# A macaron block on one core: the first stage turns most of its rows with a round trip to memory and 32x32 block transposes on VectorE, where TensorE did it

## What is computed

```
x = x + 0.5 * ffn(layernorm(x))
x = x + attn(layernorm(x))
x = x + 0.5 * ffn(layernorm(x))

ffn(y):   dots = softmax(y @ centroids.T / 0.1); hits = dots > 0.01      # 64 clusters
          query_sel = any(hits, axis=1); row_sel = any(hits, axis=0)[assignments]
          out = where(query_sel[:, None] & row_sel[None, :], y @ weight.T + bias, 0)
attn(y):  q, k, v = y @ Wq + bq, y @ Wk + bk, y @ Wv + bv                # 32 heads of 32, 8 key/value heads
          per token: scores[d, e] = sum over heads of q[d, h] k[e, h] / sqrt(32); softmax over e; times v
```

## Time and profile before

| | |
|---|---|
| median of 3 runs | 1314.02 us (1314.0 to 1318.34) |
| the profiled execution: its own time | 1314.43 us |
| its span in the profile | 1312.6 us, 21943 instructions |
| busy: PE, DVE, ACT, POOL | 1253.2, 837.8, 411.5, 437.1 us |
| share of the chain that ended last | PE 86%, DVE 9%, DMA 2% |
| moved by DMA | 178.91 MB, mean 136 GB/s |
| DMA packets under 512 bytes | 141312 of 197605 |

### The profile page before, as it was taken

The page is one execution under the profiler, slowest core; times in us unless marked ns, Lnnn a source line. Parts: engine busy times, 40 slices in busy tenths (PEclk is TensorE's granted clock), DMA queues, the critical chain, the costliest instruction groups (busy, mean ns, idle before and its releaser), DMA issues.

```text
span 1312.6 us, 21943 instructions
## 1 busy us (share of the span) xinstructions
PE 1253.2 (95%) x8776; PEld 1077.6 (82%) x8776; DVE 837.8 (64%) x1177; ACT 411.5 (31%) x590; POOL 437.1 (33%) x548
## 2 busy tenths in 40 slices
PE   5999999999999798999999999999999999979998
PEld 4788888888888677888888888888888888858887
DVE  3643343334333267888888887878888875198886
ACT  3322222222221123444344344444344443211110
POOL 1225443544231733324323433333333200051321
PEclk9999999999999898999999999999999999989999
DMA  7132333233212244555555545545545555116774
GB/s 256 53 116 89 128 108 118 89 128 100 78 65 112 73 112 112 162 153 145 146 142 132 155 132 154 164 132 147 158 123 154 137 136 187 47 67 223 271 272 177
DMA packets 197605, 178.91 MB, mean 136 GB/s; under 512 B 141312, under 2 KB 163840, under 8 KB 197504
## 3 DMA queue, kind: packets, MB, share of 16 engines
q1 hardware_dynamic: 182624, 158.11, 39.8%
q10 hardware_dynamic: 14880, 19.40, 4.3%
HBM read 103.55 MB, written 73.92 MB: 135 GB/s over the span
## 4 chain that ended last, share of the span: by engine, by line
PE 86%; DVE 9%; DMA 2%; issue 1%; POOL 1%; ACT 1%; SPq 1%; DVEq 0%; POOLq 0%
PE ps_b L257 12%; PE ps_b L259 12%; PE ps_b L258 12%; PE ps_a L257 11%; PE ps_a L259 10%; PE ps_a L258 10%; PE ps_t L264 6%; PE ps_s L1283 4%; DVE probs L1041 3%; PE ps_s L271 3%; PE ps_s L273 2%; PE ps_s L1333 2%; DVE odd_lo L992 1%; PE ps_s L278 1%; DVE qkv_tok L1036 1%
## 5 line engine op out<-in xcount | busy, mean ns | idle before, releaser
L257 PE MATMUL ps_a<-w_hi,odd_hi 128*128 128x512 f32 x464 | 187.0, 403 | 0.0
L259 PE MATMUL ps_a<-w_hi,odd_lo 128*128 128x512 f32 x464 | 182.3, 393 | 0.0
L258 PE MATMUL ps_a<-w_lo,odd_hi 128*128 128x512 f32 x464 | 182.1, 392 | 0.0
L257 PE MATMUL ps_b<-proj_hi,y_hi 128*128 128x256 f32 (+1 forms) x512 | 177.9, 347 | 0.0
L259 PE MATMUL ps_b<-proj_hi,y_lo 128*128 128x256 f32 (+1 forms) x512 | 172.6, 337 | 0.0
L258 PE MATMUL ps_b<-proj_lo,y_hi 128*128 128x256 f32 (+1 forms) x512 | 172.0, 336 | 0.0
L567 POOL TENSOR_SCALAR f_out<-f_out,token_on 128x1024 f32<-128x1024 f32 x31 | 88.6, 2857 | 173.8 <-DVE f_out L896 173.8
L291 POOL TENSOR_TENSOR var_eps<-moments,eps 128x1 f32<-128x1 f32 x96 | 18.4, 192 | 364.1 <-DVE moments L287 364.1
L613 POOL TENSOR_TENSOR f_tmp<-f_tmp,mask 128x1024 f32<-128x1024 f32 x32 | 72.7, 2273 | 146.9 <-DMA f_tmp<-f_scratch 146.9
L259 PEld LDWEIGHTS ps_b<-proj_hi,y_lo 128*128 128x128 f32 x512 | 97.1, 190 | 10.8
L896 DVE TENSOR_TENSOR f_out<-ps_b,bias_a 128x512 f32<-128x512 f32 x30 | 20.7, 691 | 132.9 <-PE ps_b L259 132.9
(11 more groups left out here) (181 smaller groups left out, 2783.1 us busy)
## 6 DMA issues: line engine op xcount, KB each, us to landing
xa<-in_L_attn_x SPq DMA_DIRECT2D x32, 512.0 KB, 5.6
f_tmp<-f_scratch SPq DMA_DIRECT2D x32, 512.0 KB, 5.0
x_ring<-in_L_attn_x SPq DMA_DIRECT2D x32, 512.0 KB, 4.2
f_scratch<-f_out SPq DMA_DIRECT2D x31, 512.0 KB, 3.0
x_scratch<-x_ring SPq DMA_DIRECT2D x30, 512.0 KB, 3.3
late<-x_scratch SPq DMA_DIRECT2D x22, 512.0 KB, 6.7
qkv_scratch<-qkv_tok SPq DMA_DIRECT2D x32, 256.0 KB, 3.0
f_scratch<-f_out ACTq DMA_DIRECT2D x60, 128.0 KB, 3.5
```

Source lines behind the costliest of these rows:

```text
L257: pe.matmul(acc, hi[:, k, :], w_h[:, k, cols], start=(k == 0), stop=False)
L258: pe.matmul(acc, hi[:, k, :], w_l[:, k, cols], start=False, stop=False)
L259: last = pe.matmul(acc, lo[:, k, :], w_h[:, k, cols], start=False, stop=(k == KB - 1))
```

## The change

Tiles 0 to 3 (`BY_PE = 4`) are turned as before. For tiles 4 to 31:

- ACT normalises in place, in `xa[t % 3]`.
- SP stores the normalised tile to a new scratch tensor `y_d` in memory (`store_normed`, 512 KB). It then waits for that store, and loads the tile back to `ya_tok[t % 2]` in four DMAs (`load_blocks`). Each moves 1024 pieces of 32 values (128 bytes), so that the 32x32 blocks of the tile change places: block row b, block column (k, a) goes to partitions 32a to 32a+31, columns (k, b).
- DVE transposes each 32x32 block in place (`turn_first`), and signals `t1`. `high_first` and `low_first` read `ya_tok` instead of `ps_t`.
- PE's `transpose_first` is gone for these tiles. ACT's `high_first` waits for the product that last read its set, since no transpose on PE stands between any more.
- On DVE the first part of the softmax moves ahead of `low_first` of the even tile.
- On SP, a tile load into `xa` now waits for the store of the normalised tile that lay there (`y_stored`), and stores and block loads are placed between the tile loads and the stores of results. The first load of stage two waits for `lo1` instead of `t1`.
- Six semaphores of stage three are shared with stage one.

```diff
+BY_PE = 4
...
+    y_d = nc.dram_tensor("y_scratch", (NT, P, EMB), F32, kind="Internal").ap()
...
+        def first_turned(t):
+            return ps_t[:, :, :] if t < BY_PE else ya_tok[t % 2][:, :].rearrange("p (k n) -> p k n", n=P)
...
                 def load_first(t):
-                    wait(sp, y1, t - 2)
+                    if t - 3 < BY_PE:
+                        wait(sp, y1, t - 2)
+                    else:
+                        sp.wait_ge(y_stored, 16 * (t - 2 - BY_PE))
                     sp.dma_start(xa[t % 3][:, :], x_d[t]).then_inc(xa_in[t % 3], 16)
...
+                def store_normed(t):
+                    sp.wait_ge(y1, t + 1)
+                    sp.dma_start(y_d[t], xa[t % 3][:, :]).then_inc(y_stored, 16)
+
+                def load_blocks(t):
+
+                    sp.wait_ge(y_stored, 16 * (t + 1 - BY_PE))
+                    if t - 2 < BY_PE:
+                        sp.wait_ge(t1, t - 1)
+                    else:
+                        sp.wait_ge(lo1, t - 1)
+                    blocks = y_d[t].rearrange("(b i) (k a j) -> a i k b j", i=D, a=T4, j=D)
+                    for a in range(T4):
+                        sp.dma_start(ya_tok[t % 2][D * a:D * a + D, :].rearrange("i (k b j) -> i k b j", b=T4, j=D),
+                                     blocks[a]).then_inc(y_in[t % 2], 16)
...
                 for p in range(NP - 1):
                     if p > 0:
                         store_first(2 * p - 1)
-                    for t in (2 * p + 5, 2 * p + 6):
-                        if t < NT:
-                            load_first(t)
+                    if 2 * p + 5 < NT:
+                        load_first(2 * p + 5)
+                    if 2 * p + 4 < NT:
+                        store_normed(2 * p + 4)
+                        load_blocks(2 * p + 4)
+                    if 2 * p + 6 < NT:
+                        load_first(2 * p + 6)
                     if 1 <= p <= KB:
                         load_proj(p - 1, [w[(p - 1) * P:p * P].rearrange("p d h -> p (d h)") for w in (Wq, Wk, Wv)])
...
                     store_first(2 * p)
+                    if 2 * p + 5 < NT:
+                        store_normed(2 * p + 5)
+                        load_blocks(2 * p + 5)
...
                 def norm_first(t):
                     act.wait_ge(norm1, t + 1)
-                    wait(act, t1, t - 1)
-                    normed(act, ya_tok[t % 2][:, :], xa[t % 3][:, :], 0, t).then_inc(y1, 1)
+                    if t < BY_PE:
+                        wait(act, t1, t - 1)
+                    to = ya_tok[t % 2] if t < BY_PE else xa[t % 3]
+                    normed(act, to[:, :], xa[t % 3][:, :], 0, t).then_inc(y1, 1)
...
                 def high_first(t):
                     act.wait_ge(t1, t + 1)
-                    act.copy(first_set(t)[0], ps_t[:, :, :]).then_inc(hi1, 1)
+                    if t >= BY_PE:
+                        act.wait_ge(ffn1[1], t - 3)
+                    act.copy(first_set(t)[0], first_turned(t)).then_inc(hi1, 1)
...
+                def turn_first(t):
+                    dve.wait_ge(y_in[t % 2], 64 * ((t - BY_PE) // 2 + 1))
+                    dve.transpose(ya_tok[t % 2][:, :], ya_tok[t % 2][:, :]).then_inc(t1, 1)
...
                 for p in range(1, NP - 2):
                     read_first(2 * p - 1, 1)
+                    turn_first(2 * p + 2)
+                    pair_soft_in(dve, p)
                     low_first(2 * p + 2)
-                    pair_soft_in(dve, p)
                     pair_soft_out(dve, 0, p)
                     stats_first(2 * p + 4)
                     read_first(2 * p, 0)
+                    turn_first(2 * p + 3)
                     low_first(2 * p + 3)
                     read_first(2 * p, 1)
                     stats_first(2 * p + 5)
                     read_first(2 * p + 1, 0)
...
                 for p in range(1, NP - 2):
-                    transpose_first(2 * p + 2)
                     fold_pair(p)
                     product_first(2 * p, 0)
-                    transpose_first(2 * p + 3)
                     product_first(2 * p, 1)
```

More of the change, by code:

```diff
@@ L220, in macaron_kernel @@
         ye, te, hie, loe = sem("ye"), sem("te"), sem("hie"), sem("loe")
-        late_in = sems("late_in", 6)
+        late_in = w_in[0:6]
         yl, tl, hil, lol = sem("yl"), sem("tl"), sem("hil"), sem("lol")
@@ L408, in _ @@
                     store_first(2 * p)
-                sp.wait_ge(t1, NT)
+                    if 2 * p + 5 < NT:
+                        store_normed(2 * p + 5)
+                        load_blocks(2 * p + 5)
+                sp.wait_ge(lo1, NT)
                 sp.wait_ge(f1_stored[0], 16)
@@ L875, in low_first @@
                     dve.wait_ge(hi1, t + 1)
-                    dve.tensor_tensor(lo, ps_t[:, :, :], hi.bitcast(F32), ALU.subtract).then_inc(lo1, 1)
+                    dve.tensor_tensor(lo, first_turned(t), hi.bitcast(F32), ALU.subtract).then_inc(lo1, 1)
                 def low_rows(j):
@@ L947, in _ @@
                     read_first(2 * p + 1, 0)
+                turn_first(NT - 2)
+                pair_soft_in(dve, NP - 2)
                 low_first(NT - 2)
-                pair_soft_in(dve, NP - 2)
                 pair_soft_out(dve, 0, NP - 2)
                 read_first(NT - 5, 1)
+                turn_first(LAST)
                 low_first(LAST)
```

5 lines of the change are left out of this document (2 added, 3 removed).

## The result

| | before | after |
|---|---|---|
| median of 8 runs, us | 1314.01 (1306.53 to 1320.15) | 1307.08 (1301.29 to 1310.77) |
| ratio of the runs | | 0.9943, 95% interval 0.9916 to 0.9969 |
| profiled execution, us (span) | 1314.43 (1312.6) | 1301.29 (1299.5) |

The change makes the kernel 6.9 us faster. 16.0 were forecast: the sign is right, and the size is less than half of what was forecast. Single executions of either kernel differ by 9 to 14 us, as much as is to be explained, so the comparison needs a point that does not carry the variation of stages two and three. I take **the mark**: the start of the first transposes of stage two on PE. All the work that the change alters lies before it; behind it only six semaphores are other ones. It stands at 439.93 us before and at 431.96 after: **8.0 us earlier**.

What follows compares the result with a forecast made beforehand. PE was taken to bound stage one, sharing the bound with the DVE, POOL, ACT chain after the change. 23.4 - 5.9 - 1.5 = 16.0 us gained, so a median of 1298.0 us, range 1293 to 1326.

Steps and rivals of the forecast that it cites:

- the likeliest case: Whole kernel: the forecast of 1298.0 us holds, own range 1293 to 1304; chance 0.5.
- the first rival, the shared read: Even tile's low part held by POOL's selection, both reading SBUF: 0.75 us in 13 rounds, 9.8 us, time 1307.8; one in four.
- What goes from PE: Eight transposes per tile leave PE's list in stage one: 1.67 us a pair, 14 pairs, 23.4 us gained.
- The wait at `pair_first`: PE waits for the odd tile's low part, 0.45 us in each of 13 rounds, 5.9 us lost.
- Start: I put 1.5 us: Loop start: tile 4's blocks arrive at 60.7, 1.1 us late, tile 5 a little too; 1.5 us lost.
- The round trip in the steady rounds: Store 3.0 us, block loads 5.3 (bounds 3.8 to 10.6), hidden by slack in steady rounds.
- its own sign: Block loads in the profile after: under 7.8 us from first issue to last landing.
- The slack of the odd tile: Rounds with projection loads: blocks at 272.8, transpose may start at 275.3; slack 2.5 us, 1.2 with the worst store.
- a sign of being wrong: DVE's block transposes waiting for `ya_tok` loads in rounds with projection loads would show the forecast wrong; no size given.
- The rival of late blocks: Odd tile's blocks land later than 7.8 us in 8 projection-load rounds; up to 1325.7 us; chance 0.25.

Runs made afterwards that it cites:

- e12: e11 with tile 5's xa load in round 0 put back ahead of tile 4's y_scratch store: median 1293.94 us, ratio 0.9817 to the kernel before.
- e1: The change without the round trip: the norm writes ya_tok directly, no store or block loads, result wrong: mark 424.24, time 1297.76 us.
- e2: The change with six tiles instead of four turned by TensorE (BY_PE = 6): mark 425.94, time 1301.44 us.
- e9: The change with only SyncE's list reordered, y_scratch store ahead of xa load, projection loads and f_scratch store: mark 426.98, time 1301.61 us.
- e3: The change with ACT's odd high part ahead of the next tile's norm from round 1 on: mark 437.90, time 1311.92 us.
- e10: The change with GpSimd's selection written as a tensor_tensor and done twice in a row: mark 462.64, time 1342.63 us.
- e4: The change with the pair logits one product later in PE's list: mark 426.55, time 1299.14 us.
- e11: The kernel of e5, timed over 6 runs: median 1297.24 us, ratio 0.9869 to the kernel before.
- e5: The change with pair logits one product later and y_scratch stores ahead in SyncE's list: mark 418.63, time 1293.73 us in one execution.
- e7: e5 with six tiles instead of four turned by TensorE: mark 418.80, time 1299.40 us.
- e8: The change with GpSimd's selection as a tensor_tensor with broadcast operand instead of a tensor_scalar: mark 430.91, time 1307.41 us.

## Why the prediction was wrong

The median of 1307.1 lies inside the range of 1293 to 1326 and outside the likeliest case's own, 1293 to 1304. That it lies next to the 1307.8 of the first rival, the shared read, is chance: that rival's wait did not occur.

- **What goes from PE: right, a little low.** 1.67 us were summed for a pair. With no wait left a round takes 24.15, 1.79 less than 25.94. e12 gets 23.3 us at the mark, where the sum had 23.4.
- **The wait at `pair_first`: right.** 0.42 where 0.45 stood, set by ACT's norm ahead of the odd high part and not by the blocks (e1 has it without any blocks). But the idle time of a row is not the wait's cost, 0.69 (24.84 - 24.15). A round is 24.84 where 25.94 - 1.22 = 24.72 stood: 13 x 0.12 = 1.6 us.
- **"Start: I put 1.5 us": this is the step that failed.** It cost 7.2. The sum looked at tile 4 and gave tile 5 "a little". Tile 4 was usable at 63.15 instead of 60.7, and tile 5, which nothing had priced, at 73.62. Three sizes in it were wrong: the store was taken at 3.0 us, the median of the earlier trace rows, and took 4.1 and 6.55; a block DMA was taken at 0.43 us of SyncE and took 0.84 here; and the 4.3 us of stall brought 2.9 more by the clock, a term that the sum did not have. Besides, tile 5's store went out 1.25 us behind its norm, because SyncE had the blocks of tile 4, a tile load and a store of results to issue first. e1 (no trip) and e2 (a later first trip) show that the trip causes this loss; e9 shows that an earlier store takes away the wait at `pair_first`, of which a part comes back at `fold_pair`.
- **The round trip in the steady rounds: close, with less slack than stated.** The forecast was 5.3 us from the first issue to the last landing; it was 5.23 to 7.95, within the bounds of 3.8 and 10.6, and once above the 7.8 that the prediction gave as its own sign. The odd tiles' stores in rounds with projection loads took 4.9 to 5.3 us where the prediction had 4.3 (263.2 to 267.5), apart from the first at 7.8. The slack of the odd tile was forecast at 2.5 us in these rounds and was 0 to 1.4. Two transposes there did wait for `ya_tok` (0.37 and 0.30), which the prediction had named as a sign of being wrong, without cost to PE; the round with the bias vectors lost 0.5 us. e3, whose even tiles start their trip 1.05 us later, has seven rounds of over 25 us.
- Together: 5.7 at the start, 1.6 in the rounds, 0.5 in one round are 7.8 of the 8.0 us between 16.0 forecast and 8.0 measured at the mark.
- **The rival of the shared read fell here** with 28 low parts of 1.22 to 1.23 us, 13 of which began under GpSimd's TENSOR_SCALAR, 2.07 us or more behind its start. The row that spoke against it (L331) and the row that spoke for it (L1041) were both true: the one lay under a TENSOR_SCALAR and the other under a TENSOR_TENSOR. I had seen in it only a short instruction against a long one. The Trainium skill, SBUF — State Buffer, section "SBUF: two separate sides", lets the lock strike against any GpSimd instruction that reads SBUF; e10 agrees for a tensor_tensor, and the 13 low parts under a tensor_scalar do not.
- **The rival of late blocks** did not decide the change. It decides the next step: e3 and e4 show that the moment anything else is freed, the round trip binds.

What stays open: why the profiled execution of the change and its median differ by 5.8 us while those of the kernel before do not. The traces say where: from the mark to the end the change's profiled execution took 867.5 us, less than each of the other thirteen (870.8 to 878.8; the kernel before 872.7). The last transposes of stage two already stand 5.4 us earlier behind the mark than in the kernel before (671.2 against 676.6). So it was a quick pass through stage two, and what makes stage two vary was not tried.

## What to carry to other kernels

A buffer trip through memory that is hidden in the steady rounds is not hidden in the first one: write its start out instruction by instruction, for each of the first tiles, with the issuing queue's own time and with what stands ahead of each store. A queue that issues in order and waits for landings is an engine with a length of its own; add up its issues and waits for a round, as one does for PE, and put the transfer that something waits for ahead of those that have slack. And when a change leaves small waits, look for the instruction whose place in the order makes them: here three moves in the order (pair logits, stores, one load), with no work removed, brought 15.4 us at the mark, where the change itself had brought 8.0.

## What the runs showed of the hardware

- Behind a wait of PE the granted clock can fall to 1.2 GHz, and this adds to the price of the wait: 2.9 us behind a wait of 4.59, 1.54 behind some waits of 2.02, nothing behind waits of 0.42. Nothing either behind 2.25 (e11) and 2.81 (e5), so the length of the wait is not all that decides.
- A block load (1024 pieces of 128 bytes to 32 partitions) holds SyncE's queue 0.68 us at the median (0.57 to 2.24 in the change, up to 5.6 in e7), one of 32 whole rows of 4 KB 0.42 (0.30 to 1.15). The number of pieces is not all of it: the loads of o_tok, also 1024 such pieces but to 128 partitions, hold it 0.38 at the median in the kernel before.
- GpSimd's multiplication by a value per row takes 1.90 us as a tensor_tensor with a broadcast operand and 2.86 as a tensor_scalar (128x1024, float32). The first holds a DVE tensor_tensor with both inputs in SBUF until it ends (e10, and L334 in e8). The second did not when the DVE instruction began 1.2 us or more behind its start; five that began earlier, in e4, took 0.1 to 0.4 us longer, with another GpSimd instruction right before. It did hold a DVE tensor_scalar (0.91 us in place of 0.16).
- What DVE reads matters too. In stage two of the kernel before, 20 low parts that read one input from PSUM began under a GpSimd tensor_tensor and took their usual 1.21 to 1.23 us. A DVE block transpose in place was held by neither kind (1.23 to 1.25).
